# A graph network on one core: queries, keys and values written out tile by tile, and four statistics buffers in the second layer

## The reference

```python
# layer 0, second of two graph attention convolutions (one head)
h = x1 @ W2
alpha = segment_softmax(leaky_relu(al_s[src] + al_d[dst]), dst)
out = segment_sum(h[src] * alpha, dst) + b2
x = _layernorm(x + out)

# layer 1, dot-product attention over the edges
q = (x @ Wq + bq).reshape(n, 8, 32)
k = (x @ Wk + bk).reshape(n, 8, 32)
v = (x @ Wv + bv).reshape(n, 8, 32)
scores = einsum('ehd,ehd->eh', q[src], k[dst]) / sqrt(32)
p = segment_softmax(scores, dst)
x = _layernorm(x + segment_sum(v[src] * p, dst))
```

## Time and profile before

| | |
|---|---|
| median of three runs | 4131.34 us (4128.31 to 4131.36) |
| the profiled execution's own time | 4160.81 us |
| its span, first to last instruction | 4159.1 us |
| mean granted TensorE clock | 0.901 |
| busy: PE, weight loads, DVE, ACT, POOL | 80%, 62%, 68%, 45%, 61% |
| instructions | 57942 |

### The profile page before, as it was taken

The page is one execution under the profiler, slowest core; times in us unless marked ns, Lnnn a source line. Parts: engine busy times, 40 slices in busy tenths (PEclk is TensorE's granted clock), DMA queues, the critical chain, the costliest instruction groups (busy, mean ns, idle before and its releaser), DMA issues. The chain is left out here.

```text
span 4159.1 us, 57942 instructions
## 1 busy us (share of the span) xinstructions
PE 3324.5 (80%) x14668; PEld 2594.7 (62%) x14668; DVE 2815.1 (68%) x7889; ACT 1860.4 (45%) x5076; POOL 2545.2 (61%) x2930
## 2 busy tenths in 40 slices
PE   4999924568677699856999995499999999999775
PEld 3888712357455455433777774387878787878654
DVE  4666645559778455586666663488888888888732
ACT  2777700047523222223333331266656666666554
POOL 4777665188567566523333331487878787878667
PEclk8999955679899899955999997699999999999998
DMA  4877707724267322256333334976767676767664
GB/s 111 236 236 237 232 9 222 243 79 129 84 194 206 91 78 77 61 155 191 90 113 109 115 115 131 298 235 202 234 197 235 201 234 198 235 201 235 186 197 156
DMA packets 709256, 705.57 MB, mean 170 GB/s; under 512 B 92630, under 2 KB 663049, under 8 KB 708702
## 3 DMA queue, kind: packets, MB, share of 16 engines
q1 hardware_dynamic: 604546, 478.91, 37.5%
q0 software_dynamic: 74752, 181.57, 15.5%
q10 hardware_dynamic: 29660, 41.70, 3.0%
HBM read 422.60 MB, written 296.47 MB: 173 GB/s over the span
## 5 line engine op out<-in xcount | busy, mean ns | idle before, releaser
L620 POOL DMA_INDIRECT s_i_messages<-h,table_row x600 | 647.0, 1078 | 191.5 <-issue 129.7
L2558 PE MATMUL s_i_bank<-s_i_messages,s_i_equal 128*128 128x256 f32 x1200 | 364.5, 387 | 81.4 <-DMA s_i_messages<-h,table_row 76.8
L801 PE MATMUL s_n_bank<-w,n_xt 128*128 128x256 f32 x1280 | 308.0, 384 | 20.5 <-DMA n_xt<-in_x_t 20.5
L2595 DVE SCALAR_TENSOR_TENSOR s_i_y<-s_i_bank,s_i_scale,s_i_acc 128x256 f32<-128x256 f32 x600 | 284.6, 475 | 44.6 <-PE s_i_bank L2558 23.5
L819 PE MATMUL s_n_bank<-w_out,n_ht 128*128 128x256 f32 x1280 | 307.8, 384 | 0.9 <-ACT n_ht L829 0.9
L810 PE MATMUL s_n_bank<-n_x3t,w_in 128*128 128x256 f32 x1280 | 305.0, 381 | 0.0
L2558 PEld LDWEIGHTS s_i_bank<-s_i_messages,s_i_equal 128*128 128x128 f32 x1200 | 218.8, 193 | 112.7 <-issue 82.5
L841 ACT ACTIVATE n_w<-n_w,n_small 128x256 f32<-128x256 f32 x320 | 145.5, 502 | 313.0 <-POOL n_small L868 277.8
L801 PEld LDWEIGHTS s_n_bank<-w,n_xt 128*128 128x128 f32 x1280 | 247.2, 193 | 55.9 <-DMA n_xt<-in_x_t 20.9
L819 PEld LDWEIGHTS s_n_bank<-w_out,n_ht 128*128 128x128 f32 x1280 | 246.1, 193 | 35.6 <-ACT n_ht L829 1.3
L810 PEld LDWEIGHTS s_n_bank<-n_x3t,w_in 128*128 128x128 f32 x1280 | 244.6, 191 | 33.8 <-ACT n_x3t L699 0.2
(11 more groups left out here) (422 smaller groups left out, 9436.1 us busy)
## 6 DMA issues: line engine op xcount, KB each, us to landing
h<-s_i_y SPq DMA_DIRECT2D x600, 128.0 KB
n_xt<-in_x_t SPq DMA_DIRECT2D x160, 256.0 KB
out<-n_w SPq DMA_DIRECT2D x160, 256.0 KB
s_i_equal<-eq_tab SPq DMA_DIRECT2D x600, 64.0 KB
x<-s_x_rows SPq DMA_DIRECT2D x100, 256.0 KB
out<-s_a_hs SPq DMA_DIRECT2D x100, 128.0 KB
proj_dst<-s_a_hd SPq DMA_DIRECT2D x100, 128.0 KB
h<-s_h_rows SPq DMA_DIRECT2D x50, 256.0 KB
```

The lines of the kernel that those rows point to most:

```text
L620: return net.nc.gpsimd.indirect_dma_start(out, None, table, bass.IndirectOffsetOnAxis(index, 0))
L801: mm = self.nc.tensor.matmul(self.pr[:, g * self.D:(g + 1) * self.D], self.XT[u][:, c, g * P:(g + 1) * P], self.net.w12[:, c, :], start=c ...
L2558: nc.tensor.matmul(banks[r % 4][:, 0:D], EQ[q % NM][:], M[q % NM][:], start=True, stop=True).then_inc(summed, 1)
L2595: V.scalar_tensor_tensor(Y[q % NY][:], banks[r % 4][:, 0:D], scale[:, s, t:t + 1], acc[:, t, :], ALU.mult, ALU.add).then_inc(added, 1)
```

## The change

In `gat2` the statistics S get four buffers instead of two, and DVE waits for the unit four back instead of two back before it writes them. Everything else there stays.

`project_qkv` is written out tile by tile, with one semaphore per kind of event instead of four:

- POOL gathers with the index columns read straight from `table_row` and `dst_row`, without copies, into six buffers X.
- PE signals after the query-value product and again after the key product, and waits for DVE's key addition of two tiles back only ahead of the key product.
- ACT moves the transposes and nothing else.
- DVE adds the key bias straight from PSUM. In turn i it adds the biases of tile i, reduces the product of tile i - 2 and multiplies tile i - 1.

```diff
-        S = st.sb("d_small", [P, 32], n=2)
+        S = st.sb("d_small", [P, 32], n=4)
...
-                    past(dve, x1_ready, k - 1)
+                    past(dve, x1_ready, k - 3)
...
-    U, TURNS = 4, T // 4
+    NX, AHEAD = 6, 4
...
-            with gp.Fori(0, TURNS) as j:
-                for u in range(U):
-                    hold(net, gp, *upto(tp, u, j, back=U))
-                    nc.gpsimd.tensor_copy(I[u][:, 0:1], col(net.table_row, j * U + u)).then_inc(idx[u], 1)
-                    nc.gpsimd.tensor_copy(I[u][:, 1:2], col(net.dst_row, j * U + u)).then_inc(idx[u], 1)
-                    hold(net, gp, *upto(idx, u, j, inc=2))
-                    for i in range(2):
-                        gather(net, X[u][:, i, :], net.x1, I[u][:, i:i + 1]).then_inc(got[u], 16)
+            for t in range(T):
+                past(gp, tp_made, t - NX + 1)
+                gather(net, X[t % NX][:, 0, :], net.x1, net.table_row[:, t:t + 1]).then_inc(got[t % NX], 16)
+                gather(net, X[t % NX][:, 1, :], net.x1, net.dst_row[:, t:t + 1]).then_inc(got[t % NX], 16)
...
+            def transposes(t):
+                if t < T:
+                    pe.wait_ge(got[t % NX], 32 * (t // NX + 1))
+                    past(pe, xt_ready, t - 1)
+                    for k in range(4):
+                        mm = nc.tensor.transpose(tps[t % 2][:, k * P:(k + 1) * P], X[t % NX][:, k // 2, (k % 2) * P:(k % 2 + 1) * P], net.ident[:])
+                    mm.then_inc(tp_made, 1)
+
+            def project(t):
+                if 0 <= t < T:
+                    b = t % 2
+                    pe.wait_ge(xt_ready, t + 1)
+                    past(pe, q_ready, t - 1)
+                    past(pe, v_ready, t - 1)
+                    for c in range(C):
+                        mm = nc.tensor.matmul(qvs[b][:, :], XT[b][:, c, :], net.w_qv[:, c, :], start=c == 0, stop=c == C - 1)
+                    mm.then_inc(queried, 1)
+                    past(pe, k_ready, t - 1)
+                    for c in range(C):
+                        mm = nc.tensor.matmul(kps[b][:, 0:D], XT[b][:, 2 + c, :], net.w_k[:, c, :], start=c == 0, stop=c == C - 1)
+                    mm.then_inc(keyed, 1)
+            for i in range(T + 1):
+                transposes(i)
+                project(i - 1)
...
+            for t in range(T):
+                act.wait_ge(tp_made, t + 1)
+                past(act, keyed, t - 1)
+                nc.scalar.activation(XT[t % 2][:].rearrange("p k e -> p (k e)"), tps[t % 2][:, :], ACT.Copy).then_inc(xt_ready, 1)
...
+            def biased(t):
+                if t < T:
+                    b = t % 2
+                    dve.wait_ge(queried, t + 1)
+                    past(dve, qk_ready, t - 1)
+                    V.tensor_tensor(Q[b][:], qvs[b][:, 0:D], bias[:, 0, :], ALU.add).then_inc(q_ready, 1)
+                    V.tensor_tensor(net.v_edge[:, t, :], qvs[b][:, D:2 * D], bias[:, 1, :], ALU.add).then_inc(v_ready, 1)
+                    dve.wait_ge(keyed, t + 1)
+                    V.tensor_tensor(K[b][:], kps[b][:, 0:D], bias[:, 2, :], ALU.add).then_inc(k_ready, 1)
...
+            for i in range(T + 2):
+                biased(i)
+                score(i - 2)
+                product(i - 1)
```

More of the change, by code:

```diff
@@ L1663, in power @@
                     p, w = rows(k)
-                    s = S[k % 2]
+                    s = S[k % 4]
                     gp.wait_ge(var, k + 1)
@@ L1734, in norm @@
                     for g in range(w):
-                        mv = nc.scalar.activation(Y[k % 3][0:p, g, :], Y[k % 3][0:p, g, :], ACT.Identity, bias=S[k % 2][0:p, 22 + g:23 + g],
-                                                  scale=S[k % 2][0:p, 20 + g:21 + g])
+                        mv = nc.scalar.activation(Y[k % 3][0:p, g, :], Y[k % 3][0:p, g, :], ACT.Identity, bias=S[k % 4][0:p, 22 + g:23 + g],
+                                                  scale=S[k % 4][0:p, 20 + g:21 + g])
                     mv.then_inc(x1_ready, 1)
@@ L1778, in join @@
                     p, w = rows(k)
-                    s, y = S[k % 2], Y[k % 3]
+                    s, y = S[k % 4], Y[k % 3]
                     ch = Chain(dve, chain, 2 * w + 1, 0)
@@ L1839, in _ @@
         @block.tensor
         def _(pe):
-            def transposes(j, u):
-                b = u % 2
-                pe.wait_ge(*upto(got, u, j, inc=32))
-                pe.wait_ge(*upto(xt, u, j, back=2))
-                for k in range(4):
-                    mm = nc.tensor.transpose(tps[b][:, k * P:(k + 1) * P], X[u][:, k // 2, (k % 2) * P:(k % 2 + 1) * P], net.ident[:])
-                mm.then_inc(tp[u], 1)
-            def project(j, u):
-                b = u % 2
-                pe.wait_ge(*upto(xt, u, j))
-                pe.wait_ge(*upto(kv, u, j, back=2))
-                pe.wait_ge(*upto(biased, u, j, back=2, inc=2))
-                for c in range(C):
-                    nc.tensor.matmul(qvs[b][:, :], XT[b][:, c, :], net.w_qv[:, c, :], start=c == 0, stop=c == C - 1)
-                for c in range(C):
-                    mm = nc.tensor.matmul(kps[b][:, 0:D], XT[b][:, 2 + c, :], net.w_k[:, c, :], start=c == 0, stop=c == C - 1)
-                mm.then_inc(pr[u], 1)
@@ L1860, in turn @@
-            def turn(j, more):
-                for u in range(U):
-                    if more or u + 1 < U:
-                        transposes(*following(U, j, u))
-                    project(j, u)
-            turns_ahead(pe, TURNS, lambda j: transposes(j, 0), turn)
+            def transposes(t):
[5 more added lines that the diff above has]
+                    mm.then_inc(tp_made, 1)
@@ L1881, in turn @@
-            def turn(j, more):
-                for u in range(U):
-                    if more or u + 1 < U:
-                        move(*following(U, j, u))
-                    keys_values(j, u)
-            turns_ahead(act, TURNS, lambda j: move(j, 0), turn)
+            for t in range(T):
+                act.wait_ge(tp_made, t + 1)
+                past(act, keyed, t - 1)
+                nc.scalar.activation(XT[t % 2][:].rearrange("p k e -> p (k e)"), tps[t % 2][:, :], ACT.Copy).then_inc(xt_ready, 1)
@@ L1890, in _ @@
             V = nc.vector
-            dve.wait_ge(bias_in, 48)
-            with dve.Fori(0, TURNS) as j:
-                for u in range(U):
-                    b = u % 2
-                    dve.wait_ge(*upto(pr, u, j))
-                    dve.wait_ge(*upto(qk, u, j, back=2))
-                    V.tensor_tensor(Q[b][:], qvs[b][:, 0:D], bias[:, 0, :], ALU.add)
-                    V.tensor_tensor(net.v_edge[:, bass.ds(j * U + u, 1), :].rearrange("p o d -> p (o d)"), qvs[b][:, D:2 * D], bias[:, 1, :],
-                                    ALU.add).then_inc(biased[u], 1)
-                    dve.wait_ge(*upto(kv, u, j))
-                    V.tensor_tensor(KV[b][:], KV[b][:], bias[:, 2, :], ALU.add).then_inc(biased[u], 1)
-                    dve.wait_ge(*upto(biased, u, j, inc=2))
-                    dve.wait_ge(*upto(sc, u, j, back=2))
-                    V.tensor_tensor(QK[b][:], Q[b][:], KV[b][:], ALU.mult).then_inc(qk[u], 1)
-                    dve.wait_ge(*upto(qk, u, j))
-                    V.tensor_reduce(net.scores[:, 0:H, bass.ds(j * U + u, 1)].rearrange("p h o -> p (h o)"), heads(QK[b][:], H), AXX, ALU.add).then_inc(sc[u], 1)
+            def biased(t):
[7 more added lines that the diff above has]
+                    V.tensor_tensor(K[b][:], kps[b][:, 0:D], bias[:, 2, :], ALU.add).then_inc(k_ready, 1)
@@ new lines, in score, with product @@
+            def score(t):
+                if 0 <= t < T:
+                    b = t % 2
+                    dve.wait_ge(qk_ready, t + 1)
+                    V.tensor_reduce(net.scores[:, 0:H, t], heads(QK[b][:], H), AXX, ALU.add).then_inc(scored, 1)
+            def product(t):
+                if 0 <= t < T:
+                    b = t % 2
+                    dve.wait_ge(q_ready, t + 1)
+                    dve.wait_ge(k_ready, t + 1)
+                    past(dve, scored, t - 1)
+                    V.tensor_tensor(QK[b][:], Q[b][:], K[b][:], ALU.mult).then_inc(qk_ready, 1)
```

25 lines of the change are left out of this document (7 added, 18 removed).

## The result

The changed kernel takes **4078.57 us** (median of 4 runs, 4075.99 to 4087.1), the kernel before 4129.83 us (4127.78 to 4131.36): ratio 0.988, 95% interval 0.9863 to 0.9897, that is 51.3 us less, between 42.5 and 56.6. The forecast was 4087 in a range of 4077 to 4106. The profiled execution of the change ran 4077.15 us around a span of 4074.7.

What follows compares the result with a forecast made beforehand. POOL's gather stream bounds the query-key-value stage, and DVE's statistics wait holds layer 2. Savings of 35.2 + 1.0 - 0.4 + 8.2 = 44.0 us from 4131.34 give 4087.3 us, range 4077 to 4106.

Steps and rivals of the forecast that it cites:

- The bound and where it moves: Query-key-value stage: POOL's gather instructions set 3.38 us per tile; after the change PE becomes the bound at 3.02 us.
- 35.2 + 1.0 - 0.4 = 35.8 us: Query-key-value stage: 35.2 us from 97 shorter tiles, 1.0 from an earlier first gather, 0.4 lost on a sixth closing DVE operation.
- The sign named for being wrong altogether: PE's granted clock falling below 0.97 in a stage that keeps it busier; no size given.
- POOL loses 2 copies per tile and the hand-over behind them: Query-key-value stage: without index copies and their hand-over to the gather, POOL's tile falls from 3.38 to some 2.5 us.
- The start: Query-key-value stage: the first gather no longer waits for two copies and the second pair follows sooner; 1 us saved.
- Layer 2: Four statistics buffers remove DVE's 0.68 us stall; 41 units go from 4.41 to 4.21 us, saving 8.2 us.
- the ring through PE: Layer 2: PE's chain of aggregate, transposes, projection, next sums and next aggregate limits each unit to 4.21 us.
- the 28.8 us: Layer 2: DVE's 41 waits before its statistics for ACT's normalizing; only 8.2 us of them was forecast to come back.
- The store ring (rival B): Layer 2: y waits for the store three units back, period stays near 4.41 us; 35.8 us saved, 4095.5; chance 0.20.
- Rival C: Query-key-value stage: PE's extra wait or DVE lengthens the tile to 3.20 us; total 4105.0 us; chance 0.10.
- Rival D: Query-key-value stage: the 0.79 us idle follows any wait, so POOL stays at 3.3 us per tile; 4114.7 us; chance 0.06.
- Rival E: Query-key-value stage: fetching straight-line code stalls PE at about 9 packets; at 6 us each, 54 us lost, 4141.3; chance 0.02.

Runs made afterwards that it cites:

- sums first: Changed kernel with PE taking layer 2's sums of the next unit ahead of the projection of the unit two back; 4114.21 us against 4146.31 before.
- the second profile: The changed kernel itself, unaltered, run again in another set beside the kernel before; 4106.53 us against 4146.31, ratio 0.9909.

## Why the prediction was right, and where it was not

**The bound and where it moves.** Right. POOL's stream set the pace, PE's 3.02 us took over, no DVE, no extra wait and no signal stood in the way. The terms of this stage, 35.2 + 1.0 - 0.4 = 35.8 us, are 37.6 in the first profile. In the second they are 29.9, since 8 us of standstill go off them. The sign named for being wrong altogether, a granted clock under 0.97 in this stage, did not come: 0.98 in the first profile, 0.97 with the standstill.

**What of POOL's 3.38 us was dear.** The sum is right, its reason is not. The step "POOL loses 2 copies per tile and the hand-over behind them" prices both together, and credits the copies. The runs split it: the copies and their hand-over may stay. What mattered was a separate instruction after the wait, 0.52 us per tile, which the listing of the order shows between copy and gather (`L177 ISA`), and which I had put down to the hand-over without a row for it. It was one mechanism with one place, and a look for the idle of a gather behind a plain wait in other stages would have parted them.

**The start.** Priced 1 us. From SP's first issue to the first gather it was 1.51 us (the earlier trace rows and 1403.03) and is 0.71 (1363.77 to 1364.48): 0.8 us. What the forecast lacked is the standstill some 20 us in.

**Layer 2.** Forecast 8.2 us; 8.5 within one set, 11.5 between the first two profiles, where the one of before holds the late store of the earlier trace rows and two more late units. The reason is confirmed by sums first: with the ring through PE broken, DVE shows 3.71 us. It was also right that only a part of the 28.8 us would come back.

**The store ring (rival B).** Did not decide, in part by luck. The forecast carried the 5.70 us between a y and the store over to the new period, which left 2.72 us for a landing. It fell to 5.49 and left 2.93. The stores that were waited for took 2.75 and 3.37 us in the change and 2.60 to 4.17 in sums first, their median 2.77, so with 2.72 us more of them could have been late. The Trainium skill, page "DMA: Bandwidth & Descriptors", section "Anatomy of one DMA", has a fit for transfers issued by GpSimd that gives an estimated 2.60 us for this size; these stores are SyncE's, and the shortest that was waited for took just that. At 3.7 us per unit that ring does decide, as the 17 waits show.

**Rival C** did not come: 3.01 us with the extra wait and without. **Rival D** held that an idle of 0.79 us might belong to the first gather behind any wait. A gather behind a plain wait on POOL's own copies has 0.27, so it does not. But its doubt about the copies was justified: the idle stayed with the form of the wait, and the change relieved POOL because it dropped that form. **Rival E**: no loss at every fetched packet, the last 91 tiles take 274.3 us in every written-out kernel. But in seven of those eight profiles something stops PE early on, once or twice, and costs 6 to 9 us, a sixth of the gain. That is a loss of the size of a seventh of E's 54 us; no instruction packet is seen in the stops, and their cause stays open.

**The numbers.** Forecast 44.0 us, measured 51.3 (42.5 to 56.6) in the first comparison and 39.8 (30 to 46) in the second. The forecast lies between them, in the interval of both, for partly offsetting reasons: layer 2 and the tiles a little better, the start worse in the second profile. That the sum came out although its reason for POOL's excess was wrong is no accident: whatever made the excess, PE's 3.02 us was the next bound, and the change took all of it away.

## What to carry to other kernels

An idle spell marked "issue" before an instruction that reads fresh data has two possible owners, the hand-over and whatever else stands between the two instructions; read the order of the program there before choosing, and try the smaller edit. Here two edits, four statistics buffers and POOL's plain waits, gave what the whole rewrite gave. When a stall goes, count the next two rings, not one: here DVE's wait hid PE's ring, and PE's ring hid the stores and the table loads, so that a step freed of PE's ring made the stage 8 us longer (257.3 us against 249.2). A stage that nothing touches can differ by 20 us between chips and executions, so compare stages and not spans.

## What the runs showed of the hardware that I had not expected

- On GpSimd a wait followed by a separate count costs 0.52 us more ahead of an indirect DMA than the same wait on the DMA itself (0.79 against 0.27 us of idle).
- The DVE operation that weighs the equality tables got faster by itself. Group rows of layer 2, before and after the change, same form, same work:

```profile
L1751 DVE TENSOR_SCALAR s_d_equal<-s_d_equal,scores 128x128 f32<-128x128 f32 x100 | 33.0, 370 | 7.1 <-DMA s_d_equal<-eq_tab 7.1
```

```profile
L1751 DVE TENSOR_SCALAR s_d_equal<-s_d_equal,scores 128x128 f32<-128x128 f32 x100 | 23.9, 283 | 6.7 <-DMA s_d_equal<-eq_tab 6.6
```

  It now runs at another moment of POOL's turn. The Trainium skill, page "Advanced Engine Details and Errata", section "GPSIMD Details", says that GpSimd shares a read and a write interface with VectorE; the rows fit that, and no run here tests it. In the profile before, 40 of the 100 operations meet POOL's power (L1666) and take 456 ns in the mean, the other 60 take 313; in the change none meets it, and the mean is 283. DVE has slack there, so it bought nothing.
- PE's results came 5.5 us after the end that its records are given, near the start of a stage, with the granted clock at 0.50 from 1418.3 to 1425.0 us. The Trainium skill, page "Runtime: NRT & Kernel Launch", section "Instruction fetch mechanics", calls the cost of fetching straight-line code mostly hidden, and a taken branch the danger; in these runs seven of eight profiles of the written-out stage stand still and none of the looped one does, whatever the cause.
- The stage of layer 1's gather took 158 to 183 us over the profiles here with the same code.
